# Four-layer convolution kernel: stores, loads and sign writes by ScalarE, late channel statistics by VectorE

## The reference

```python
def _L0_conv_ref(x, w1, b1, w2, b2):          # layers 2 and 3 alike
    pooled = x.mean(axis=(2, 3))
    hdn = jax.nn.relu(pooled @ w1 + b1)
    kernels = (hdn @ w2 + b2).reshape(b, NK, K, K)
    ...                                        # depthwise 3x3, padding 1
def _L1_conv_ref(x, W):
    xb = ste_sign(x)
    wb = ste_sign(W)
    ...                                        # dense 3x3, padding 1
def _gn(v, G=16, eps=1e-5):                    # 16 groups of 2 channels
    ...
x = x + _L0_conv_ref(_gn(x), ...)
x = x + _L1_conv_ref(_gn(x), L1_conv_W)
x = x + _L2_conv_ref(_gn(x), ...)
x = x + _L3_conv_ref(_gn(x), ...)
```

## Time and profile before

| | us |
|---|---|
| median of 3 runs | 4339.41 (4338.14 to 4343.95) |
| the profiled execution | 4362.16 |
| its span, first to last instruction | 4360.3 |
| PE busy | 3266.8 (75%) |
| DVE, ACT, POOL busy | 2071.6, 1784.8, 1956.4 |
| moved by DMA | 829.51 MB, mean 190 GB/s |

### The profile page before, as it was taken

How to read it: one execution, slowest core, us unless ns; L and a number is a source line. 1 busy time by engine, 2 the same in 40 slices (tenths; PEclk the granted TensorE clock), 3 DMA queues, 4 the chain that set the end, 5 groups by cost and what they waited for, 6 DMA issues and landing times.

```text
span 4360.3 us, 70554 instructions
## 1 busy us (share of the span) xinstructions
PE 3266.8 (75%) x26592; PEld 2091.4 (48%) x26592; DVE 2071.6 (48%) x6038; ACT 1784.8 (41%) x2626; POOL 1956.4 (45%) x3175
## 2 busy tenths in 40 slices
PE   0676987769876787777886787866877769777698
PEld 0443545435454454544455454553545536445355
DVE  2627643266432754337543384424744257432573
ACT  2443633336343463435434354343542436424232
POOL 1326544265433654346442564326543265332754
PEclk9988998889988898888988899988999889888899
DMA  6388697876969669596786967869778697786946
GB/s 210 58 149 169 147 318 198 155 163 153 337 166 176 163 184 327 130 213 143 198 299 123 212 153 219 288 106 211 148 227 280 105 209 159 236 268 106 205 79 218
DMA packets 589273, 829.51 MB, mean 190 GB/s; under 512 B 489731, under 2 KB 490502, under 8 KB 572550
## 3 DMA queue, kind: packets, MB, share of 16 engines
q1 hardware_dynamic: 323200, 734.28, 66.4%
q10 hardware_dynamic: 216582, 76.68, 8.2%
...
## 4 chain that ended last, share of the span: by engine, by line
PE 42%; DMA 24%; SPq 11%; DVE 8%; ACT 5%; ACTq 4%; POOL 4%; issue 3%; DVEq 0%; POOLq 0%
PE acc L979 24%; PE acc L996 12%; SPq L327 9%; DMA arena<-x 6%; DMA out<-y 6%; DMA dense_out<-arena 5%; POOL y L510 3%; DMA arena<-signs 3%; PE acc L1058 3%; ACT arena L599 2%; ACTq L606 2%; DMA signs<-arena 2%; ACTq L535 2%; DVE dense_stats L860 1%; DMA arena<-y 1%
## 5 line engine op out<-in xcount | busy, mean ns | idle before, releaser
L979 PE MATMUL acc<-y,arena 64*128 64x384 f32 x9216 | 1726.5, 501 | 179.9 <-ACT y L568 146.1
L979 PEld LDWEIGHTS acc<-y,arena 64*128 64x128 f32 x9216 | 1014.0, 194 | 739.2 <-ACT y L568 230.6
L327 POOL DMA_DIRECT2D arena<-y x1536 | 790.6, 522 | 836.7 <-PE acc L996 725.4
L996 PE MATMUL acc<-arena 64*128 64x384 f32 x4608 | 958.4, 509 | 226.3 <-issue 208.9
L568 ACT ACTIVATE y<-acc 128x768 f32<-128x768 f32 x832 | 644.4, 808 | 1177.0 <-PE acc L996 1176.1
L489 POOL TENSOR_SCALAR arena<-arena,cst,fill 128x24 f32<-128x24 f32 (+1 forms) x1536 | 613.7, 419 | 710.7 <-issue 469.8
L510 POOL TENSOR_TENSOR y<-arena,y 128x3072 f32<-128x3072 f16 x88 | 529.9, 6045 | 735.0 <-DMA arena<-dense_out 734.9
L860 DVE BATCH_NORM_STATS2 dense_stats<-y 128x6 f32<-128x192 f32 x1536 | 408.0, 344 | 729.2 <-POOL y L510 728.9
L996 PEld LDWEIGHTS acc<-arena 64*128 64x128 f32 x4608 | 525.1, 196 | 450.7 <-issue 240.9
L1058 PE MATMUL acc<-arena,wd_side 128*32 128x384 fp8e4 (+1 forms) x10752 | 471.8, 330 | 287.1 <-DMA arena<-signs 234.6
L802 DVE TENSOR_SCALAR_CACHE_REDUCE y<-acc 128x768 f32<-128x768 f32 x256 | 245.1, 958 | 640.3 <-PE acc L996 640.3
...
## 6 DMA issues: line engine op xcount, KB each, us to landing
y<-x SPq DMA_DIRECT2D x64, 2304.0 KB, 27.1
out<-y SPq DMA_DIRECT2D x64, 2304.0 KB, 22.9
arena<-y SPq DMA_DIRECT2D x768, 141.0 KB
arena<-x SPq DMA_DIRECT2D x168, 576.0 KB, 6.5
dense_out<-arena ACTq DMA_DIRECT2D x384, 192.0 KB, 7.0
...
arena<-y SPq DMA_DIRECT2D x768, 71.9 KB
...
```

The costliest lines, as they stand in the source:

```text
L327: eng.dma_start(halo[at:at + n, slot, :, d0:d0 + size], y[source:source + (n - 1) * step + 1:step, first + odd:first + odd + 3:2, s0:s0 + ...
L979: nc.tensor.matmul(acc[:, 2 * k + odd, 0:KN], w_center[at, slot, 2 * q + odd, :], y[at, 2 * g + odd, k * KN:(k + 1) * KN], start=turn == 0 ...
L996: nc.tensor.matmul(acc[:, 2 * k + odd, 0:KN], w_halo[at, slot, q, :], halo[at, bt % HALO_SLOTS, q, k * KN:(k + 1) * KN], start=False, stop ...
```

## The change

The order of work on PE stays. What moves:

- `evictor`: in layer 3 ACT evicts all three thirds of every pair; DVE evicts only in layer 0.
- Stores and loads go by pairs (1152 KB, a semaphore for each pair), and ACT issues them: the store right behind a pair's eviction, the load `load_next` of pair 0 and 1 three pairs after its store, of the others seven pairs after it (`LOAD_WITH`), so that the loads of pairs 9 to 15 are issued in pairs 0 to 6 of the next layer 0. ACT waits for `stored` before each.
- ACT also writes the signs, right behind the batch's second pair.
- Channels ahead: 28 (before 24). ACT keeps 16 in layer 2. DVE takes four in layer 2 (with pairs 2, 6, 10, 13), eight in layer 3 (pairs 0 to 7), and channels 0 to 3 from `y` in pairs 10 and 11. A third slot lies in `dense_stats`. SP issues the channels of layer 2 and the first three late ones, ACT the other five, in pairs 1 to 5 of layer 3.
- SP keeps the halos, the sign loads and the loads of layer 1's result.
- `signs` is declared as half as many float16; the bytes are the same.

```diff
-AHEAD_FIRST = 8
-AHEAD = C - AHEAD_FIRST
-AHEAD_SLOTS = 2
-AHEAD_LATE = AHEAD - PAIRS
+AHEAD_FIRST = 4
+AHEAD_ACT = [(AHEAD_FIRST + i, i % 2) for i in range(PAIRS)]
+AHEAD_WITH = [2, 6, 10, 13]
+AHEAD_DVE = [(AHEAD_FIRST + PAIRS + n, 2) for n in range(len(AHEAD_WITH))]
+AHEAD_LATE = [(AHEAD_FIRST + PAIRS + len(AHEAD_WITH) + n, (0, 2, 1)[n % 3]) for n in range(8)]
+AHEAD = AHEAD_ACT + AHEAD_DVE + AHEAD_LATE
+AHEAD_SLOTS = 3
+ARRIVE_WITH = 10
+DVE_AHEAD = C - len(AHEAD_ACT)
+LOAD_WITH = [g + (3 if 2 * g < AHEAD_FIRST else 7) for g in range(PAIRS)]
...
 def act_channels(s, li):
     if li == 0:
-        return [c for c in range(C) if c % BATCH_CH < 2] if s == 0 else list(range(AHEAD_FIRST, C))
+        return [c for c in range(C) if c % BATCH_CH < 2] if s == 0 else [c for c, _ in AHEAD_ACT]
 def dve_channels(s, li):
-    return [c for c in range(C) if c not in act_channels(s, li)]
+    if li == 0:
+        return [c for c in range(C) if c % BATCH_CH >= 2] if s == 0 else []
+    return list(range(C))
...
 def evictor(d, g, k):
-    if d % ND == 0:
-        return "act" if k == 1 else "dve"
-    return "dve" if d % ND == 2 and k == 0 and g < AHEAD_LATE else "act"
+    return "dve" if d % ND == 0 and k != 1 else "act"
...
-        signs = nc.dram_tensor("signs", [P, C, STAGED], F8, kind="Internal").ap()
+        signs = nc.dram_tensor("signs", [P, C, STAGED // 2], F16, kind="Internal").ap()
...
-        ahead = part(A_STAGE, AHEAD_SLOTS * N * 4, F32).rearrange("p (k n) -> p k n", k=AHEAD_SLOTS)
+        ahead = [part(A_STAGE + k * N * 4, N * 4, F32) for k in range(2)] + [dense_stats[:].rearrange("p c w s -> p (c w s)")]
+        sign_pairs = [part(A_SIGN + k * SIGN_BYTES, SIGN_BYTES, F16) for k in range(2)]
...
-        loaded = [sem(f"loaded{b}") for b in range(BATCHES)]
-        stored = [sem(f"stored{b}") for b in range(BATCHES)]
+        loaded = [sem(f"loaded{g}") for g in range(PAIRS)]
+        stored = [sem(f"stored{g}") for g in range(PAIRS)]
...
+        def wait_ahead(eng, s, entry):
+            slot = entry[1]
+            order = [e for e in AHEAD if e[1] == slot]
+            eng.wait_ge(ahead_in[slot], 16 * (s * len(order) + order.index(entry) + 1))
+        def load(eng, s, g):
+            at = slice(2 * g, 2 * g + 2)
+            eng.dma_start(y[:, at, :].rearrange("p c n -> p (c n)"),
+                          x[s, :, at].rearrange("p c g w -> p (c g w)")).then_inc(loaded[g], 16)
+        def store(eng, s, g):
+            wait_evicted(eng, (s * ND + ND - 1) * PAIRS + g + 1)
+            at = slice(2 * g, 2 * g + 2)
+            eng.dma_start(out[s, :, at].rearrange("p c g w -> p (c g w)"),
+                          y[:, at, :].rearrange("p c n -> p (c n)")).then_inc(stored[g], 16)
+        def load_next(eng, s, g):
+            eng.wait_ge(stored[g], 16 * (s + 1))
+            load(eng, s + 1, g)
+        def load_ahead(eng, s, entry):
+            if s < B - 1:
+                c, slot = entry
+                order = [e for e in AHEAD if e[1] == slot]
+                at = order.index(entry)
+                if at > 0 and order[at - 1] in AHEAD_ACT:
+                    eng.wait_ge(act_stat, stat_count(act_channels, s, 0) + AHEAD_ACT.index(order[at - 1]) + 1)
+                elif at > 0:
+                    eng.wait_ge(dve_ahead, s * DVE_AHEAD + (AHEAD_DVE + AHEAD_LATE).index(order[at - 1]) + 1)
+                eng.dma_start(ahead[slot], x[s + 1, :, c].rearrange("p g w -> p (g w)")).then_inc(ahead_in[slot], 16)
...
-            def load(s, b):
-                at = slice(b * BATCH_CH, (b + 1) * BATCH_CH)
...
-            def store(s, b):
-                wait_evicted(sp, ((s * ND + ND - 1) * BATCHES + b + 1) * BATCH_PAIRS)
...
-            def load_ahead(s, i):
-                    if i >= AHEAD_SLOTS:
-                        sp.wait_ge(act_stat, stat_count(act_channels, s, 0) + i - AHEAD_SLOTS + 1)
...
-            def write_signs(s, b):
-                sp.wait_ge(sign_ready, s * PAIRS + (b + 1) * BATCH_PAIRS)
...
                 for b in range(BATCHES):
-                    if b > 0:
-                        write_signs(s, b - 1)
-                write_signs(s, BATCHES - 1)
                 first += BATCHES
-                for b in range(HALO_SLOTS):
+                halos(first)
+                load_ahead(sp, s, AHEAD_ACT[0])
+                load_ahead(sp, s, AHEAD_ACT[1])
+                for b in range(1, HALO_SLOTS):
                     halos(first + b)
-                for i in range(AHEAD_SLOTS):
-                    load_ahead(s, i)
+                sp.wait_ge(means_ready, s * ND + 2)
+                load_ahead(sp, s, AHEAD_DVE[0])
                 for b in range(BATCHES):
-                    load_ahead(s, 2 * b + AHEAD_SLOTS)
+                    if b < BATCHES - 1:
+                        load_ahead(sp, s, AHEAD_ACT[2 * b + 2])
                     halos(first + b + HALO_SLOTS)
-                    load_ahead(s, 2 * b + AHEAD_SLOTS + 1)
+                    if b < BATCHES - 1:
+                        load_ahead(sp, s, AHEAD_ACT[2 * b + 3])
+                    if b in (1, 3, 5):
+                        load_ahead(sp, s, AHEAD_DVE[b // 2 + 1])
+                    if b == BATCHES - 1:
+                        load_ahead(sp, s, AHEAD_LATE[1])
+                        load_ahead(sp, s, AHEAD_LATE[0])
                 first += BATCHES
+                load_ahead(sp, s, AHEAD_LATE[2])
                 for b in range(BATCHES):
                         halos(first + b + HALO_SLOTS)
-                    for i in range(2):
-                        load_ahead(s, PAIRS + AHEAD_SLOTS + 2 * b + i)
-                    store(s, b)
-                    if s < B - 1:
-                        if b > 0:
-                            sp.wait_ge(stored[b - 1], 16 * (s + 1))
-                            load(s + 1, b - 1)
-                        if b == BATCHES - 1:
-                            sp.wait_ge(stored[b], 16 * (s + 1))
-                            load(s + 1, b)
-            for b in range(BATCHES):
-                sp.wait_ge(stored[b], 16 * B)
+            for g in range(PAIRS):
+                sp.wait_ge(stored[g], 16 * B)
...
+                if s > 0:
+                    pool.wait_ge(dve_ahead, s * DVE_AHEAD - AHEAD_FIRST)
...
                 last.then_inc(sign_ready, 1)
+                if g % BATCH_PAIRS == BATCH_PAIRS - 1:
+                    act.wait_ge(sign_ready, s * PAIRS + g + 1)
+                    first = A_STAGE + (b % 2) * STAGE_BYTES
+                    src = part(first, STAGE_BYTES, F16)[:, 0:BATCH_CH * STAGED // 2]
+                    for a in range(2):
+                        to = signs[a * 64:(a + 1) * 64, b * BATCH_CH:(b + 1) * BATCH_CH, :]
+                        act.dma_start(to.rearrange("(i j) c n -> j i (c n)", j=S), src[a:P:2, :])\
+                            .then_inc(sign_out[b % 2], 16)
...
                     evict(d, g)
+                    if s > 0 and PAIRS + g in LOAD_WITH:
+                        load_next(act, s - 1, LOAD_WITH.index(PAIRS + g))
                         pair_signs(s, g - 1)
...
                     evict(d + 2, g)
+                    store(act, s, g)
-                        if g < AHEAD_LATE:
-                            ahead_stats(s, PAIRS + g)
+                        if g in LOAD_WITH:
+                            load_next(act, s, LOAD_WITH.index(g))
+                        if 3 <= g + 2 < len(AHEAD_LATE):
+                            load_ahead(act, s, AHEAD_LATE[g + 2])
                             root(d + 3)
...
-            def channel_stats(c):
+            def channel_stats(c, src, done):
-                dve.sem_inc(dve_stat, 1)
+                dve.sem_inc(done, 1)
+            def ahead_stats(s, entry):
+                c, slot = entry
+                wait_ahead(dve, s, entry)
+                channel_stats(c, ahead[slot], dve_ahead)
...
+                    if li == 1 and s < B - 1 and g in AHEAD_WITH:
+                        ahead_stats(s, AHEAD_DVE[AHEAD_WITH.index(g)])
-                        if AHEAD_LATE <= g < AHEAD_LATE + AHEAD_FIRST // 2:
-                            for c in (2 * (g - AHEAD_LATE), 2 * (g - AHEAD_LATE) + 1):
-                                dve.wait_ge(loaded[c // BATCH_CH], 16 * (s + 2))
-                                channel_stats(c)
+                        if g < len(AHEAD_LATE):
+                            ahead_stats(s, AHEAD_LATE[g])
+                        elif ARRIVE_WITH <= g < ARRIVE_WITH + AHEAD_FIRST // 2:
+                            dve.wait_ge(loaded[g - ARRIVE_WITH], 16 * (s + 2))
+                            for c in (2 * (g - ARRIVE_WITH), 2 * (g - ARRIVE_WITH) + 1):
+                                channel_stats(c, y[:, c], dve_ahead)
...
+                if li == 0 and s > 0:
+                    pe.wait_ge(dve_ahead, s * DVE_AHEAD)
```

55 lines of the change are left out of this document (22 added, 33 removed).

## The result

| | before | after |
|---|---|---|
| median of the runs (20 of each) | 4338.77 (4317.53 to 4354.74) | 4314.63 (4295.86 to 4343.95) |
| the profiled execution's span | 4360.3 | 4310.7 |
| moved by DMA | 829.51 MB | 846.06 MB |

The ratio is 0.9946, with a 95% interval of 0.9929 to 0.9962: 24 us faster, where 225 were predicted. The time lies outside the predicted range.

The account below looks back on a forecast made before the run. Full DMAs for 130 us, then one queue's order starving them while PE waits, were taken to bound layer 3 and the next layer 0. Gains 210 + 3 + 10 + 3 = 226 us gave 4114 us, range 3985 to 4290.

Parts of the forecast that it names:

- What bounds the kernel: Layer 3 and next layer 0: 63 us excess, seven times, from full DMAs for 130 us and one queue's order.
- The chain behind the 13.07 us: Layer 0: PE's wait "for issue" was traced from the border to POOL, to halos, to a load; 13.07 us.
- The floor, "46 us": Layer 3 and next layer 0: at least 208 us by bytes, 224 by DMA share; gain 54 or 38, taken as 46.
- What is late next: Layer 3 and next layer 0: DMA backlog delays sign writes, late channels and borders, costing 16 us a sample.
- Stores and loads out of SP's queue: Layer 3 and next layer 0: SP no longer waits for evictions and stores; 46 - 16 = 30 us per sample, 210 us.
- k = 0 by ACT: Start of layer 3: ACT evicts instead of DVE; 3 us in eight layers, only the eighth added separately, 3 us.
- DVE and layer 2: Layer 2: 3 us won by earlier channels, 1.5 lost at its end; +1.5 us a sample, 10 us for seven.
- Ends: Span's end and start: a last store half as large gains 3 us; the start could gain 15, taken as 0.
- B: Layer 3 and next layer 0: DMAs are the bound, 13 us gained per sample, 4232 us (4205 to 4320); chance 0.17.
- C: Whole kernel: only issue time is saved, SP's issues are not the bound, no change, 4339 us; chance 0.04.
- A: Layer 3 and next layer 0: all order stalls go, 380 to 460 us gained, 3880 to 3960 us; chance 0.11.
- D: Layer 3 and next layer 0: ACT stands behind DMAs, slower at 4465 us, decided from 48 us of landing; chance 0.11.

Follow-up runs that it names:

- e6: Changed kernel with every halo copy of SP and POOL moving half its elements, same number of copies: 3882.73 us, ratio 0.8943 to the kernel before.
- e1: Changed kernel with the five late channels that ACT issued in layer 3 issued by SP, ahead of its halos: 4246.81 us, ratio 0.9774.
- e2: Changed kernel with each batch's signs written by SP behind the halos, no longer by ACT: 4369.08 us, ratio 1.006.
- e17: Changed kernel with halo rows spread four partitions apart and late channels issued by SP, behind the same batch's halos: 4190.47 us, ratio 0.9649.
- e10: e1 with layer 0's halos copied from x in DRAM instead of y, so they wait for no load: 4230.63 us, ratio 0.9744.
- e5: Kernel before with the evictor edit alone, ACT evicting k = 0 of pairs 0 to 7 of layer 3 too: 4314.94 us, ratio 0.9942.

## Why the prediction was wrong, point by point

*What bounds the kernel.* Place and symptoms were read rightly: the excess lies in layer 3 and the next layer 0. From before to e6 L3 shrinks by 30.5 and L0 by 31.7 us a sample, 62 together, where the first part gave 63 as the excess; layer 2 shrinks by 3. The text saw "two causes at once" and gave 46 of the 63 us to the order of the queue. The runs give the greater part to what the copies cost the DMAs: 432 us for halved halos, where the rearranged queues were worth nothing in sum and single moves of order 54 to 74 us either way (e1, e2, e17). The chain behind the 13.07 us, "hence a load", was only read off: with the load's wait taken away, e10 gains 16 us in seven samples.

*The floor, "46 us".* This term of the sum failed. It held bytes at 329 GB/s, or DMA share, for a floor that the changed kernel would nearly reach, since the DMAs would stay full up to pair 6 of layer 0. Its two stretches take 255 us in sample 1 where 208 to 224 was the floor. The DMA line of the window 1050 to 1305:

```profile
DMA packets 13703, 57.79 MB, mean 227 GB/s; under 512 B 5330, under 2 KB 5330, under 8 KB 9589
```

The bytes are those that were reckoned (58.3), but not the rate. By share the DMAs did as much as before, 0.82 x 123 + 0.68 x 132 = 191 us (188 before), and they did not stay full. Two windows of after, the first with PE standing before DVE's weights, show why:

```profile
1100.00:1110.00 10.00, 0.52 (x4) 0.00 (x0) 2.83 (x9) 1.43 (x2) 5.28 (x13) 0.66 1.02 285
1120.00:1130.00 10.00, 6.30 (x28) 3.63 (x30) 6.39 (x20) 2.32 (x3) 0.36 (x1) 0.66 0.25 104
```

First full DMAs hold back the late channel and with it PE; then PE has made nothing to store, ACT issues no store between 1101.54 and 1129.30, and the DMAs run empty at a share of 0.25. The floor was reckoned as if the DMAs never had to wait for PE. Its rate is no better: one taken over a mixed stretch can't price its parts. A MB of stores was worth 1.2 us of the kernel's time, of rows 4.3, of sides 6.1, where 3.0 was put for each. Nor is the DMA share a fixed amount of work: spreading took 230 us from it at equal bytes.

*"What is late next", 16 us.* The backlog was counted as 4 MB after pair 5, 6 to 12 us before a late channel; measured were medians of 26.5 and 28.8 us from issue to landing, and 12 to 36 in sample 1, against 11.6 us of slack. The same count put the halos down as 0.44 MB a pair, 1.3 us; at e6's 170 GB/s they are 2.6. "Up to 3 us" for the late channels was 16.66 us of PE's time in sample 1 (10.28 + 6.38), and 68 / 7 = 9.7 us a sample by e1, which also issues two of them sooner. The term was in the list, with the right link (two pairs of slack), and was sized by a rate that didn't hold; this is the second failure. The sign write of 9 to 12 us came out (12.21). But its successors of 4.61 and 6.27 us were not foreseen.

*Stores and loads out of SP's queue, 30 us a sample.* In the profiles L3 and L0 together are 8.3 us a sample shorter (145.3 + 121.5 less 137.7 + 120.8), and 4.0 of that the evictor alone gives (e5: 141.9 + 120.9). By the medians, which agree for e5 and after, this step was worth nothing. With the halos halved the same step measures 20.4 us a sample with the evictor's 3, so 17: not 30 even with room. So 46 - 16 = 30 was wrong in both of its terms.

*k = 0 by ACT.* Right: 3 us in eight layers, 24 us, and e5 measures 24. The first matmuls of layer 3 no longer stand before DVE's eviction.

*DVE and layer 2, +1.5 us a sample.* Not seen: the sum of eight layers 2 is 875.6 us before and 873.7 after, and between the kernels of the study it wanders from 849 to 883. *Ends.* The last store ends the span 4.6 us after its issue (4306.10 to 4310.7) where it was 7.3: right, 3 us. But layer 3 of sample 7 has a border pause of 5.16 us that it didn't have, and takes 108.1 instead of 102.5 us. Perhaps ACT's stores, now by pairs and without a wait, meet the halos there too; no run shows it. The start didn't move.

*The rivals.* B, the DMAs as the bound, came nearest in its mechanism and its sign (DVE idle before L758 for 7.38 and 16.58 us in layer 3 of sample 1). The 4315 lies in the case that it reached for, 4205 to 4320, but its 4232 was 83 us too low, as it built on the same floor by share. C's number was nearest, 24 us off. These 24 us are the evictor's, which C didn't have, and its zero for the queues is right only in sum. The Trainium skill has the rule behind it ("DMA: Bandwidth & Descriptors", "Issuing engines are not separate DMA queues"), that issuing from several engines saves the issue time alone. The total agrees with it, since e5 alone gives the same time as the whole change; single moves between the queues don't, since e1 won 68 us (in part by an earlier issue) and e2 lost 54. A's time was reached by e6 alone, D's nowhere: loads landed in 33.0 us, under its 48.
